# Unread matrix products in TensorE's idle time at the opening of layer 0

## What is computed

```python
x = x + _L0_xattn_ref(_layernorm(x), ctx_1024, ctx_1024, Wq, Wk, Wv, Wo)   # 16 heads of 8, rotary q and k
x = x + _L0_ffn_ref(_layernorm(x), W1, b1, W2, b2)                          # 128 -> 512 -> 128, ternary weights
x = x + _L1_xattn_ref(_layernorm(x), ctx_1024, ctx_1024, mask, ...)         # grouped queries, masked
x = x + _L1_ffn_ref(_layernorm(x), wg_red, wg, w1, b1, w2, b2)              # one of 8 experts for each token
```

## Time and profile before

| what | value |
|---|---|
| median of three runs | 529.06 us (527.42, 529.06, 530.39) |
| profiled execution, its own time | 524.59 us |
| its span, first to last instruction | 522.8 us |
| mean granted clock of TensorE over the span | 0.967 |
| TensorE, matmul busy | 451.3 us, 86% of the span |
| VectorE busy | 378.1 us, 72% |
| ScalarE busy | 348.4 us, 67% |
| GpSimd busy | 336.9 us, 64% |
| TensorE busy in us 0 to 5, 5 to 10, 10 to 15, 15 to 20, 20 to 25, 25 to 30 | 0, 0.66, 4.32, 2.65, 2.75, 2.57 us |

### The profile page before, as it was taken

The page is one execution under the profiler, slowest core; times in us unless marked ns, Lnnn a source line. Parts: engine busy times, 40 slices in busy tenths (PEclk is TensorE's granted clock), DMA queues, the critical chain, the costliest instruction groups (busy, mean ns, idle before and its releaser), DMA issues.

```text
span 522.8 us, 19052 instructions
## 1 busy us (share of the span) xinstructions
PE 451.3 (86%) x6127; PEld 349.3 (67%) x6127; DVE 378.1 (72%) x1113; ACT 348.4 (67%) x892; POOL 336.9 (64%) x710
## 2 busy tenths in 40 slices
PE   2567999999987888998799999999988719999992
PEld 2345777777766777997456666665655409999991
DVE  6788988888888557874557888888998663555551
ACT  4357788888876455665267788888876824666660
POOL 5798887788763345856445665888887780555552
PEclk9999999999999999999789999999999957999997
DMA  7557454545551720353212232333331234444430
GB/s 182 145 144 176 117 138 122 141 127 146 130 136 35 245 45 1 74 110 101 55 49 73 70 76 66 89 106 86 102 93 58 69 123 112 105 106 107 108 99 20
DMA packets 99107, 53.43 MB, mean 102 GB/s; under 512 B 25234, under 2 KB 96034, under 8 KB 99026
## 3 DMA queue, kind: packets, MB, share of 16 engines
q1 hardware_dynamic: 95666, 45.06, 34.9%
q0 software_dynamic: 2784, 6.82, 3.7%
q10 hardware_dynamic: 576, 0.53, 0.3%
HBM read 17.89 MB, written 8.81 MB: 51 GB/s over the span
## 4 chain that ended last, share of the span: by engine, by line
PE 63%; DVE 10%; DMA 8%; issue 6%; POOL 6%; SPq 3%; ACT 2%; ACTq 0%; DVEq 0%; POOLq 0%
PE bank L739 9%; PE bank L966 7%; PE score L687 6%; PE scoreT L956 4%; PE bank L874 4%; DMA stack<-negpT 4%; DVE negmax L1609 3%; PE scoreT L864 3%; DMA stack<-pieces 3%; PE bank L788 3%; PE score L652 3%; PE bank L601 3%; PE score L956 2%; PE scoreT L662 2%; PE scoreT L714 2%
## 5 line engine op out<-in xcount | busy, mean ns | idle before, releaser
L1609 DVE TENSOR_REDUCE negmax<-score 128x8 f32<-128x1024 f32 x128 | 156.4, 1222 | 41.5 <-PE score L687 40.4
L1081 ACT ACTIVATE P<-scoreT 128x1024 f32<-128x1024 f32 x128 | 131.2, 1025 | 46.4 <-PE scoreT L705 26.1
L739 PE MATMUL bank<-P,Vc 128*32 128x128 f32 x2048 | 69.8, 277 | 1.7 <-issue 1.5
L1523 POOL DMA_INDIRECT out<-by x39 | 37.3, 957 | 46.7 <-DVE by L1969 45.7
L739 PEld LDWEIGHTS bank<-P,Vc 128*32 128x32 f32 x2048 | 52.6, 110 | 15.6 <-issue 12.5
L687 PE MATMUL score<-stack 64*128 64x128 bf16 x896 | 44.9, 220 | 8.9 <-DMA stack<-pieces 4.4
L687 PEld LDWEIGHTS score<-stack 64*128 64x128 bf16 x896 | 25.6, 95 | 38.0 <-issue 22.7
L1362 POOL TENSOR_TENSOR negp<-negmax,blank 128x16 bf16<-128x16 f32 x64 | 14.1, 220 | 53.5 <-DVE negmax L1609 51.9
L966 PE MATMUL bank<-M,P 128*128 x312 | 41.4, 276 | 1.0 <-DVE by L1969 0.5
L1254 ACT ACTIVATE P<-scoreT,We 128x128 f32<-128x128 f32 x104 | 29.8, 371 | 15.0 <-PE scoreT L956 15.0
L966 PEld LDWEIGHTS bank<-M,P 128*128 128x128 f32 x312 | 38.0, 192 | 1.3 <-issue 1.3
(11 more groups left out here) (222 smaller groups left out, 1212.4 us busy)
## 6 DMA issues: line engine op xcount, KB each, us to landing
stack<-pieces SPq DMA_DIRECT2D x96, 128.0 KB, 2.6
stack<-pieces SPq DMA_DIRECT2D x96, 64.0 KB
XB<-expert_rows SPq DMA_DIRECT2D x39, 66.0 KB, 1.9
XA<-expert_rows SPq DMA_DIRECT2D x39, 64.0 KB
XR<-in_x SPq DMA_DIRECT2D x4, 512.0 KB, 4.7
ctxT<-in_ctxT SPq DMA_DIRECT2D x16, 128.0 KB, 2.4
stack<-blank SPq DMA_DIRECT2D x32, 64.0 KB, 2.1
stack<-negpT SPq DMA_DIRECT2D x64, 32.0 KB, 1.9
```

What stands on the lines that cost most here:

```text
L739: mm = nc.tensor.matmul(PVOUT[VCOL * i:VCOL * (i + 1), half * 128:(half + 1) * 128], Vc[:, k % BODY, at:at + VCOL], P32[:, 2 * p_slot(L, k ...
L1081: nc.scalar.activation(P32[:, at:at + 2, :], SCORET[:], ACT.Exp, scale=SCALE).then_inc(sem("exp_done"), 1)
L1523: nc.gpsimd.indirect_dma_start(out=out, out_offset=bass.IndirectOffsetOnAxis(ap=at_, axis=0), in_=by[r][:, 0:D], in_offset=None).then_inc( ...
L1609: nc.vector.tensor_reduce(negmax[:, k % 2, :, half * HQ:(half + 1) * HQ], SCORE[:].rearrange("p r (h k) -> p r h k", h=HQ), AX.X, ALU.max, ...
```

## The change

TensorE's stream gets a wait for the first `ones_set` at its head, and 18 products of `ones` with `ones` into the first 128 columns of bank 7, all ahead of the wait for the first loads. A helper `unread(n)` makes n products of `ones` and `eye` into `OUTP`, a part of bank 7 that the first real output projection (step 2) overwrites. It is called in four steps: 7 products in step -4, after the v projection and before the k projection of pair 1; 5 in step -3, after the v projection and before the q projection of pair 2; 8 in step -1, at the end, after the q projection of pair 3; 6 in step 1, at the end, after the q projection of pair 4. In all 44 products are added. Nothing is removed or moved, and no other engine's stream changes.

```diff
--- before.py
+++ after.py
@@ -57,6 +57,7 @@
 REGION = TOKENS + 128
 TURNS = 3
 WARM = 12
+FIRST_WARM, IDLE = 18, {-4: 7, -3: 5, -1: 8, 1: 6}
 SLOTS_OF_P = 3
 UNITS = ((0, 6), (6, 12), (12, 18), (18, 22), (22, 26), (26, 28), (28, 30), (30, 32))
 UNIT_AT = {end + 3: n for n, (_, end) in enumerate(UNITS)}
@@ -555,6 +556,9 @@
 
         @block.tensor
         def _(pe):
+            pe.wait_ge(sem("ones_set"), 1)
+            for _ in range(FIRST_WARM):
+                nc.tensor.matmul(bank[7][:, 0:128], ones[:], ones[:], start=True, stop=True)
             pe.wait_ge(sem("first_loaded"), FIRST_LOADED)
 
             def quantize_sums():
@@ -811,6 +815,11 @@
                                      sums[:].unsqueeze(1).broadcast_to([128, m, EXPERTS]),
                                      start=False, stop=True, skip_group_check=True).then_inc(sem("ranked"), 1)
 
+                def unread(n):
+
+                    for _ in range(n):
+                        nc.tensor.matmul(OUTP, ones[:], eye[:], start=True, stop=True)
+
                 def step(t, j):
                     scores(t + 2, 0, j + 2)
                     scoresT(t, 0, j)
@@ -824,6 +833,8 @@
                         xn_transposes(j + 7, t)
                     if L == 0:
                         project_v(t + 4, j + 4)
+                    if L == 0 and isinstance(t, int) and t in (-4, -3):
+                        unread(IDLE[t])
                     scores(t + 2, 1, j + 2)
                     scoresT(t, 1, j)
                     out_project(t - 2, j - 2)
@@ -834,6 +845,8 @@
                     elif L == 0:
                         project_q(j + 7, 0)
                         project_q(j + 7, 1)
+                        if isinstance(t, int) and t in (-1, 1):
+                            unread(IDLE[t])
                     elif j % 2 == 0:
                         base_logits(j + 6)
                         project_q(j + 6, 0)
```

## The result

The changed kernel took 533.95 us at the median (531.33 to 537.40, four executions) against 528.60 for the kernel before (four executions beside them), a ratio of 1.0128, interval 1.0079 to 1.0178. The forecast was 527.8, and the range ended at 531.0. Two later comparisons, twelve executions of the changed kernel each, gave 1.0040 (1.0001 to 1.0080) and 1.0069 (1.0034 to 1.0103). So it is slower, and by something between 0.4 and 1.3%. The ratios leave out the few executions that came out slow, and are not the quotient of the two medians, from which they differ by up to 0.33% in what follows.

What follows compares the result with a forecast made beforehand. TensorE, busy 86% of the span, was taken as the bound for most of the kernel. From the median 529.06, -1.5 (burst), +1.75 (eight) and -1.5 (clock) gave 527.8 us, no measurable change; range 523.8 to 531.0.

Steps and rivals of the forecast that it cites:

- The burst and the head start: 18 products before the first loads raise TensorE's clock early, ending by 8.0 us; -1.5 us, bounds 0 and -1.9.
- The seven, the five and the six: Products in steps -4, -3 and 1 fit idle gaps of 2.22, 1.22 and 1.43 us; nothing, or a tenth.
- The eight in step -1: Behind pair 3's q projection, no gap: they delay batch 2's scores and what follows; +1.75 us, bounds 0 and 1.86.
- the clock in an ordinary execution: Opening: products in gaps may keep a clock that would otherwise fall; -1.5 us taken, bounds 0 and -3.2.
- the first (usually low before, steady after): Opening's clock usually low before, steady after: 526.1 us, or 524.4 if the eight fit; 0.36 with the latter's better half.
- The second (the eight are free): Step -1's eight cost nothing, pair 2's pieces being late otherwise: 527.6 or 526.1 us; chance split between 0.57 and 0.36.
- The fourth (no head start): TensorE's stream starts late or the clock rises after 8.94, yet the eight cost: 530.8 us; within the forecast's 0.57.
- The third: Clock doesn't rise in the burst, or falls before the first transposes and stays low: +7.2 us, or 536; chance 0.07.

Runs made afterwards that it cites:

- the eight in both places: The change plus eight more products in the idle time ahead of the first maxima's transpose, keeping the eight ending step -1; 538.79 us against 537.39 before, ratio 1.0023.
- the gap kernel: The change with its eight products of step -1 moved into the idle time ahead of the first maxima's transpose; ratios 0.9968, 0.9985 and 0.9950 to the kernel before.

## Why the prediction was wrong

**The burst and the head start** were right: -1.5 us worked out, -1.48 measured at the q projection of pair 2, and the k cast at 13.58 where 13.79 was expected. The burst ended at 8.10 against "by 8.0".

**The seven, the five and the six** cost nothing, as worked out.

**The eight in step -1** were right in place, and in size up to batch 2. The delay alone, with the clock held, is 1.57 us at batch 2 (31.02 against 29.45), where +1.75 was put down, and the net of both terms, +0.05 against 30.97, where +0.25 was. What stands behind them in the three streams was named, and batch 4 was late. But the chain as traced brought only 0.45 us to the issue of the pieces; the rest of the lag of 2.47 came in their landing behind the load, which the sum gave no term. Farther on the eight cost more than 1.75: with the clock held and the eight in both places 1.0023 against 0.9968 for the gap kernel, about 2.9 us on two different chips.

**The step that failed is "the clock in an ordinary execution".** The prediction credited the products in the gaps with a clock that stays up, and took -1.5 us for it. Its list of idle gaps, 2.22, 1.22 and 1.43 us, left out the widest, the one ahead of the first transpose of the maxima. In the timeline of TensorE of the kernel before it reads:

```profile
28.37 0.22 PE L762 MATMUL bank<-eyeb,negp 128*128 128x128 bf16 x1 [2.23 <-issue]
```

This gap of 2.23 us gets nothing from the change, while the eight products of the same step stand behind it. In all three profiles of the change the clock fell there (0.72 from 26 to 32), and the slow projection and slow first products came on top of the delay: scores of batch 2 at 32.47, 32.68 and 32.18, so 1.2 to 1.7 us later than with the clock held (31.02). The kernel before loses 1.15 us at the same point when its clock falls (32.12 against 30.97). So in place of -1.5 the term came to between nothing and +0.5, though from single profiles of different chips.

It was too large on the other side as well. A low clock in the opening before was priced at 3.2 us and measured 0.98 at batch 4 and 2.0 at the sixty-first maximum. Part of the slower work ran in idle time, and a group of scores took 0.61 us for 0.40, where the price had 0.33 more for each of three. The profile of before was rightly called a lucky one, but the opening makes 1 to 2 of the 4.5 us by which it lay under the median. Nor did the credit come in full where the clock held: for the gap kernel, with the head start and without the delay, the same sum gives -3.0 us, and its three ratios give -1.7, -0.8 and -2.6.

This step is 1.5 to 2.0 us of the 6.2 by which 533.95 missed 527.8, and of the 3.4 and 4.9 by which the later ratios did (531.2 and 532.7 on 529.06). The rest lies in the landing of the pieces and in what is open below.

**Of the rivals,** the first (usually low before, steady after) had its first half right, as far as two profiles say, and its second wrong. The second (the eight are free) fell: they delay batch 2 by 1.57 us, and eight more delay it again. The fourth (no head start) fell with the burst's end at 8.10. The third, slower by a clock that doesn't hold, is the nearest; it had the fall ahead of the first transposes and priced all four places at 7.2 us, with a chance of 0.07. The fall came later and in one place, which it didn't list.
**What is open.** The opening accounts for 2.5 us at batch 4 in the first profile and for 3.5 from batch 15 on, with the clock's second fall. Why the last piece took 6.4 us to land there, and 5.7 and 5.5 in the other two profiles of the change, isn't shown beyond the load in front of it. In those two the lag behind the first profile of the kernel before is 2.4 and 2.0 us at the sixty-first maximum, and the second profile of the kernel before itself has 2.0 there too. The rest of the 6.7 us came in late stages that the change doesn't touch; the lag of other kernels moves there by some us too (from the sixty-first maximum to the hundred and twenty-first, the gap kernel's second profile from -0.6 to +2.2, and the kernel before in its second from +2.0 to +5.4). Whether a shifted start causes this or chance does wasn't told apart, and so it stays open why the first four executions gave 1.0128 and twelve others 1.0040 and 1.0069. Why TensorE's clock fell in one profile of the kernel before and not in the other, under the same instructions, is not shown either.

## What to carry to other kernels

Filler work belongs ahead of the wait that it is to fill, not at the end of the step in which the wait stands: in an in-order stream a few lines decide between a gap and the path, here 5 us of 530 on the one chip that ran both. Before crediting filler with a clock, list every idle time of the stretch, and see that the widest one has got some. And read a second profile of the kernel before when its own time lies off the median.

## What the runs showed of the hardware

The clock fell to 1.2 GHz in stretches where TensorE was never idle for longer than 2.3 us: ahead of 28.55 in the changed kernel, and at 18.33 in the second profile of the kernel before, behind an idle time of 2.04 us. The same stretch of the same instructions kept 2.4 GHz in another execution. With these two idle times filled down to 0.4 us or less, the granted clock was at or above 0.99 in all three profiles of the gap kernel from 14 to 50 us. The rise itself came at different times: the 36 records of the burst took between 5.62 and 7.22 us in thirteen profiles. In the gap kernel's third profile, where they took 5.62 and TensorE then idled 2.18 us, the first q projection still took 1.14 us and the k projection behind it 1.88: the clock fell again at about 10.9 (mean 0.67 from 9 to 14). That is close to the fall that the third rival named, but it didn't stay low: the seven products of step -4, at 15.07, took 1.72 us again. And chips differ: the kernel before took 529 us on two and 537 on two others.
